# Tiles 2 and 3 turned by VectorE, h in three float32r passes, the sums of T on GpSimd, and a reordered start of a residual conditioning kernel

## The reference

```python
# x (128, 128, 512), cond (128, 512), weight_matrix (1024, 512), W_proj (512, 512), b_proj (512,)
u = gelu(cond @ W_proj + b_proj, approximate=False)
W_u, W_e = weight_matrix[:512], weight_matrix[512:]
out = x + (u @ W_u)[:, None, :] + einsum('bnd,dc->bnc', x, W_e)
```

## Time and profile before

| | |
|---|---|
| time, median of 3 runs | 346.73 us (346.72 to 347.13) |
| time of the profiled execution | 347.7 us, its span 345.4 us |
| TensorE busy | 339.6 us, 98% of the span |
| TensorE weight loads | 328.7 us, 95% |
| VectorE / ScalarE / GpSimd busy | 261.7 / 247.0 / 277.2 us (76 / 72 / 80%) |
| DMA | 70.64 MB, mean 205 GB/s |
| granted TensorE clock | 1.00 in every stretch |

### The profile page before, as it was taken

The page is one execution under the profiler, slowest core; times in us unless marked ns, Lnnn a source line. Parts: engine busy times, 40 slices in busy tenths (PEclk is TensorE's granted clock), DMA queues, the critical chain, the costliest instruction groups (busy, mean ns, idle before and its releaser), DMA issues.

```text
span 345.4 us, 7856 instructions
## 1 busy us (share of the span) xinstructions
PE 339.6 (98%) x2706; PEld 328.7 (95%) x2706; DVE 261.7 (76%) x301; ACT 247.0 (72%) x424; POOL 277.2 (80%) x196
## 2 busy tenths in 40 slices
PE   7999999999999999999999999999999999999996
PEld 3758999999999999999999999999999999999996
DVE  2869977788777778877777897777789777778811
ACT  3646877877777787777778777777877777787741
POOL 0357998888989888898988889898888989888860
PEclk9999999999999999999999999999999999999999
DMA  7998697888799788879978887997887799788116
GB/s 257 331 180 236 123 238 201 221 194 204 176 228 241 195 219 196 198 180 229 237 200 218 195 197 178 232 233 202 219 197 197 175 235 237 197 209 210 83 56 228
DMA packets 72264, 70.64 MB, mean 205 GB/s; under 512 B 2880, under 2 KB 67392, under 8 KB 68032
## 3 DMA queue, kind: packets, MB, share of 16 engines
q1 hardware_dynamic: 72256, 70.53, 80.5%
HBM read 36.96 MB, written 33.55 MB: 204 GB/s over the span
## 4 chain that ended last, share of the span: by engine, by line
PE 89%; DVE 1%; ACT 0%; issue 0%
PE banks L743 30%; PE banks L747 29%; PE banks L745 29%; DVE work L509 1%; DVE banks L509 0%; DVE banks L552 0%; ACT snap_rows L461 0%; ACT y L504 0%; ACT hi L399 0%
## 5 line engine op out<-in xcount | busy, mean ns | idle before, releaser
L743 PE MATMUL banks<-t_hi,hi 128*128 128x256 f32 x496 | 140.5, 283 | 0.2 <-ACT snap_rows L461 0.2
L745 PE MATMUL banks<-t_lo,hi 128*128 128x256 f32 x496 | 140.4, 283 | 0.0
L747 PE MATMUL banks<-t_hi,lo 128*128 128x256 f32 x496 | 140.4, 283 | 0.0
L743 PE MATMUL banks<-w_hi,hi 128*128 128x256 f32 x372 | 105.3, 283 | 0.4 <-ACT banks L424 0.4
L745 PE MATMUL banks<-w_lo,hi 128*128 128x256 f32 x372 | 105.3, 283 | 0.0
L747 PE MATMUL banks<-w_hi,lo 128*128 128x256 f32 x372 | 105.3, 283 | 0.0
L509 DVE STREAM_TRANSPOSE work<-quad_raw 128x1024 f32<-128x1024 f32 (+1 forms) x62 | 100.7, 1624 | 3.6 <-DMA quad_raw<-in_x 3.6
L743 PEld LDWEIGHTS banks<-t_hi,hi 128*128 128x128 f32 x496 | 95.2, 192 | 0.6 <-issue 0.6
L747 PEld LDWEIGHTS banks<-t_hi,lo 128*128 128x128 f32 x496 | 95.2, 192 | 0.0
L745 PEld LDWEIGHTS banks<-t_lo,hi 128*128 128x128 f32 x496 | 95.2, 192 | 0.0
L316 POOL TENSOR_TENSOR lo<-work,hi 128x1024 fp32r<-128x1024 f32 x31 | 74.8, 2413 | 21.7 <-ACT hi L391 21.7
(11 more groups left out here) (71 smaller groups left out, 401.7 us busy)
## 6 DMA issues: line engine op xcount, KB each, us to landing
out<-y SPq DMA_DIRECT2D x31, 1024.0 KB, 4.5
quad_raw<-in_x SPq DMA_DIRECT2D x120, 256.0 KB, 5.7
head_raw<-in_x SPq DMA_DIRECT2D x2, 512.0 KB, 5.7
w_e<-in_L_cond_weight_matrix SPq DMA_DIRECT2D x2, 512.0 KB, 6.2
w_proj_sb<-in_L_cond_W_proj SPq DMA_DIRECT2D x1, 1024.0 KB, 10.0
w_u<-in_L_cond_weight_matrix SPq DMA_DIRECT2D x1, 1024.0 KB, 12.3
quad_raw<-in_x SPq DMA_DIRECT2D x8, 128.0 KB, 9.5
out<-y SPq DMA_DIRECT2D x3, 256.0 KB, 2.1
```

The source lines that it names most:

```text
L743: pe.matmul(psum[:, t, :], a_hi[:, 2 * j + t, :], b_hi[:, j, :], start=False, stop=False, skip_group_check=True)
L745: pe.matmul(psum[:, t, :], a_hi[:, 2 * j + t, :], b_lo[:, j, :], start=False, stop=False, skip_group_check=True)
L747: last = pe.matmul(psum[:, t, :], a_lo[:, 2 * j + t, :], b_hi[:, j, :], start=False, stop=(j == T - 1), skip_group_check=True)
```

## The change

- **Loads.** Tiles 2 and 3 are no longer loaded by one DMA of 4 KB rows behind W_e, but by four DMAs in 512-byte pieces (`second`), behind cond and W_proj. W_proj is loaded in two halves.
- **Turning.** Tiles 2 and 3 are turned by VectorE straight into PSUM (`turn_second`); TensorE's eight flips of them are gone.
- **h.** `cond_t @ W_proj` in float32 becomes three float32r passes of four matmuls each. ScalarE casts `proj_hi` (four) and `cond_hi`, VectorE makes `proj_lo` (four) and `cond_lo`; they lie in the buffers hi[0] and lo[0], so the first casts of quad 0 wait for `h_summed`.
- **GpSimd.** The identity is added to three of the four diagonals by GpSimd, and the four sums of T are made by GpSimd, after `proj_lo`. `split_t(3)` moves behind the first split of `prepare`.
- **VectorE.** S3 of quad 0 goes ahead of S2, the lo part of S1 behind the bias; `turn_up` of quad 1 goes between the two evacuations. The bias copy waits for `a_seeded`.
- **ScalarE.** `seed_a` of quad 0 reads the bias from PSUM and goes ahead of `hi_s2`, `seed_c` ahead of `hi_s3`. In `period(0)` `seed_c` of quad 1 goes behind `snap5`, and `hi_s1` of quad 1 behind `snap2`.
- **TensorE.** One more warm-up matmul; the hi·hi matmuls of tiles 0 and 1 run one j ahead. The result banks are dealt out otherwise: quad 0's A bank is now bank 7 and its C bank is bank 6.

```diff
-WARM_UP = 6
+WARM_UP = 7
...
+        proj_hi, proj_lo = of_proj(hi[0]), of_proj(lo[0])
+        cond_hi, cond_lo = of_cond(hi[0]), of_cond(lo[0])
...
+        direct = head_raw[:, 0:T * TILE].rearrange("p (n d) -> p n d", n=T)
+        second = head_raw[:, T * TILE:HEAD * TILE].rearrange("p (m n w) -> p m n w", m=NM, n=T)
...
-        a_bank = [bank(6).rearrange("p (t c) -> p t c", t=T), bank(2).rearrange("p (t c) -> p t c", t=T)]
-        c_bank = [bank(1).rearrange("p (t c) -> p t c", t=T), bank(3).rearrange("p (t c) -> p t c", t=T)]
+        a_bank = [bank(7).rearrange("p (t c) -> p t c", t=T), bank(2).rearrange("p (t c) -> p t c", t=T)]
+        c_bank = [bank(6).rearrange("p (t c) -> p t c", t=T), bank(3).rearrange("p (t c) -> p t c", t=T)]
...
+            return w_e[:, j, :].rearrange("p (a r) -> p a r", r=NJ)[:, :, j]
...
-            load_direct(0)
+            sp.dma_start(direct, x[:, 0:T, :]).then_inc(direct_loaded, 16)
             for n in range(2):
                 load_w_e(n)
-            load_direct(1)
             sp.dma_start(cond_sb[:, :], cond).then_inc(cond_loaded, 16)
-            sp.dma_start(w_proj_sb[:, :, :], w_proj_dram).then_inc(w_proj_loaded, 16)
+            for n in range(2):
+                sp.dma_start(w_proj_sb[:, 2 * n:2 * n + 2, :],
+                             w_proj_dram[:, 2 * n:2 * n + 2, :]).then_inc(w_proj_loaded[n], 16)
+            for q in range(NQ):
+                sp.dma_start(second[Q * q:Q * (q + 1)], x_dram[q, :, :, T:HEAD, :]).then_inc(second_loaded, 16)
...
+            pool.wait_ge(ident_ready, 1)
+            for j in range(1, NJ):
+                pool.wait_ge(w_e_loaded[j // 2], 16)
+                diag = diagonal(j)
+                pool.tensor_tensor(diag, diag, ident[:, :], ALU.add).then_inc(w_diag_ready, 1)
...
-            for n in range(4):
-                split_t(n)
+            b_of = w_e[:, :, :].rearrange("p (e j) (h c) -> p e h j c", e=2, h=2)
+            b11, b12, b21, b22 = b_of[:, 0, 0], b_of[:, 0, 1], b_of[:, 1, 0], b_of[:, 1, 1]
+            pool.wait_ge(proj_lo_ready, NJ)
+            pool.wait_ge(w_diag_ready, NJ - 1)
+            pool.wait_ge(first_diag_ready, 1)
+            pool.tensor_tensor(t_sum[:, 0, :, :], b12, b11, ALU.subtract).then_inc(t_summed, 1)
+            pool.tensor_tensor(t_sum[:, 2, :, :], b22, b12, ALU.subtract).then_inc(t_summed, 1)
+            pool.wait_ge(t_summed, 1)
+            pool.tensor_tensor(t_sum[:, 1, :, :], b22, t_sum[:, 0, :, :], ALU.subtract).then_inc(t_summed, 1)
+            pool.wait_ge(t_summed, 3)
+            pool.tensor_tensor(t_sum[:, 3, :, :], b21, t_sum[:, 1, :, :], ALU.subtract).then_inc(t_summed, 1)
...
                 if first:
+                    split_t(3)
                     split_s2()
                     sum_s4()
                 else:
@@ -341,6 +377,8 @@
...
+            for n in range(3):
+                split_t(n)
             prepare(0, 0, True)
...
-                act.wait_ge(direct_flipped, n + 1)
+                if n < T:
+                    act.wait_ge(direct_flipped, n + 1)
+                else:
+                    act.wait_ge(second_turned, n - T + 1)
...
             for n in range(T):
                 direct_hi(n)
             for j in range(1, NJ):
-                act.wait_ge(w_diag_ready, j + 1)
+                act.wait_ge(w_diag_ready, j)
                 act.copy(w_hi[:, j, :], w_e[:, j, :]).then_inc(w_hi_ready[j], 1)
-            for n in range(T, HEAD):
-                direct_hi(n)
+            for j in range(NJ):
+                act.wait_ge(w_proj_loaded[j // 2], 16)
+                act.copy(proj_hi[:, j, :], w_proj_sb[:, j, :]).then_inc(proj_hi_ready, 1)
+            act.wait_ge(cond_flipped, 1)
+            act.copy(cond_hi, flip_psum).then_inc(cond_hi_ready, 1)
...
             hi_t(0)
-            act.wait_ge(cond_flipped, 1)
-            act.copy(cond_t[:, :, :], flip_psum).then_inc(cond_ready, 1)
-            for n in range(1, 4):
-                hi_t(n)
+            for n in range(T, HEAD):
+                direct_hi(n)
             act.wait_ge(h_summed, 1)
             act.copy(h[:, :], h_psum).then_inc(h_ready, 1)
+            hi_t(1)
             act.wait_ge(h_flipped, 1)
             act.wait_ge(b_proj_loaded, 16)
             for j in range(NJ):
                 last = act.activation(u_t[:, j, :], flip_psum[:, j, :], ACT.Gelu, bias=b_proj_sb[:, j:j + 1])
             last.then_inc(u_ready, 1)
+            hi_t(2)
+            hi_t(3)
...
+                elif p == 0:
+                    act.wait_ge(h_summed, 1)
...
             def seed_a(k, p, first):
+                source = bias
+                if not first:
+                    act.wait_ge(c21_out, k - 1)
+                elif p == 0:
+                    act.wait_ge(h_ready, 1)
+                    act.wait_ge(bias_summed, 1)
+                    source = bias_psum
+                else:
+                    act.wait_ge(bias_ready, 1)
+                    act.wait_ge(evacuated, HEAD_CHUNKS)
+                act.copy(a_bank[p], source[:, left].unsqueeze(1).to_broadcast([P, T, H])).then_inc(a_seeded, 1)
...
+            def seed_c(k, p, first):
...
                 early = first and p == 0
+                if ahead and not early:
+                    seed_c(k + 1, 1 - p, early)
                 if ahead:
-                    seed_c(k + 1, 1 - p, early)
                     up(k + 1, 1 - p, early)
...
                 if ahead:
+                    if early:
+                        seed_c(k + 1, 1 - p, early)
                     seed_a(k + 1, 1 - p, early)
-                    hi_s1(k + 1, 1 - p, early)
+                    if not early:
+                        hi_s1(k + 1, 1 - p, early)
                 act.wait_ge(m6_done, k + 1)
                 if not first:
                     act.wait_ge(c12_out, k - 1)
                 act.copy(snap2[p][:, :, :], a_bank[p]).then_inc(snap2_taken, 1)
+                if ahead and early:
+                    hi_s1(k + 1, 1 - p, early)
...
             hi_a22(0, 0, True)
+            seed_a(0, 0, True)
             hi_s2(0, 0, True)
+            seed_c(0, 0, True)
             hi_s3(0, 0, True)
-            seed_a(0, 0, True)
-            seed_c(0, 0, True)
...
+            def turn_second(t):
+                transpose(direct_psum[t].rearrange("p j (i m) -> p m j i", m=NM),
+                          second[:, :, t, :].rearrange("p m (k j) -> p m j k", k=Q)).then_inc(second_turned, 1)
...
-            dve.wait_ge(w_diag_ready, 1)
+            dve.wait_ge(w_e_loaded[0], 16)
+            first_diag = diagonal(0)
+            dve.tensor_tensor(first_diag, first_diag, ident[:, :], ALU.add).then_inc(first_diag_ready, 1)
+            dve.wait_ge(first_diag_ready, 1)
             dve.tensor_copy(w_hi[:, 0, :], w_e[:, 0, :]).then_inc(w_hi_ready[0], 1)
             split_direct(0)
-            add_identity(1)
             split_direct(1)
-            add_identity(2)
-            add_identity(3)
             for j in range(NJ):
                 split_w(j)
-
-            b_of = w_e[:, :, :].rearrange("p (e j) (h c) -> p e h j c", e=2, h=2)
-            b11, b12, b21, b22 = b_of[:, 0, 0], b_of[:, 0, 1], b_of[:, 1, 0], b_of[:, 1, 1]
-            dve.wait_ge(w_diag_ready, NJ)
...
+            for j in range(NJ):
+                dve.wait_ge(proj_hi_ready, j + 1)
+                dve.tensor_tensor(proj_lo[:, j, :], w_proj_sb[:, j, :], proj_hi[:, j, :].bitcast(F32),
+                                  ALU.subtract).then_inc(proj_lo_ready, 1)
+            dve.wait_ge(cond_hi_ready, 1)
+            dve.tensor_tensor(cond_lo, flip_psum, cond_hi.bitcast(F32), ALU.subtract).then_inc(cond_lo_ready, 1)
+            dve.wait_ge(second_loaded, LOADS)
+            dve.wait_ge(direct_lo_ready, T)
+            for t in range(T):
+                turn_second(t)
             for n in range(T, HEAD):
                 split_direct(n)
             turn_up(0, 0, True)
             turn_low(0, 0, True)
             sum_s1(0, 0, True)
+            sum_s3(0, 0, True)
             sum_s2(0, 0)
-            split_s1(0, 0)
-            sum_s3(0, 0, True)
+            dve.wait_ge(a_seeded, 1)
             dve.wait_ge(bias_summed, 1)
             dve.tensor_copy(bias[:, :], bias_psum).then_inc(bias_copied, 1)
             dve.wait_ge(bias_copied, 1)
             dve.tensor_tensor(bias_step[:, :], bias_psum[:, right], bias[:, left], ALU.subtract).then_inc(bias_ready, 1)
+            split_s1(0, 0)
             evacuate(0)
+            turn_up(1, 1, True)
             evacuate(1)
-            turn_up(1, 1, True)
...
+            def high(j):
+                pe.wait_ge(w_hi_ready[j], 1)
+                for t in range(T):
+                    if j == 0:
+                        pe.wait_ge(direct_hi_ready, t + 1)
+                    product(t, x_hi[0], w_hi, j, first=(j == 0))
...
+            high(0)
             for j in range(NJ + 1):
+                if j + 1 < NJ:
```

(54 more changed lines are left out.)

27 lines of the change are left out of this document (5 added, 22 removed).

## The result

The changed kernel takes 345.77 us (median of 8 runs, 345.43 to 346.81) against 346.70 us before (8 runs); the ratio of the two is 0.997, 95% interval 0.9956 to 0.9984: it is 0.3% faster, where I forecast no change.

A forecast was written before the change was run, and what follows sets the result against it. TensorE, gapless from m7 of quad 0, was taken to bound the kernel. Loads +1.68 us and order -1.53 us gave +0.15 us on the 346.73 median: 346.9 us, likeliest case 346.1 to 347.4, 8-in-10 range 345.6 to 347.7.

The forecast's parts named there:

- Steady part and tail untouched, the end moves with m7 of quad 0: TensorE runs without a gap from product m7 (old start counted as 36.77 us); the end moves as much as m7.
- TensorE done with tile 3 between 27.2 and 28.4: TensorE's start-up list: 1.4 us shorter, less up to 1.2 us from GpSimd's additions meeting VectorE; 28.66 before.
- The path from T to m6, 9.13 us: Quad 0, from VectorE's start on its lower half, through casts, GpSimd's S4 and ScalarE's copy, to TensorE's product m6.
- The order's gain of 1.53 us: Start of quad 0: with the old loads, the new order of work would start m7 1.53 us earlier.
- The price of the loads on the path, 1.68 us: Queue ahead of quad 0: 1.12 us for slower 512-byte pieces plus 0.56 us for a changeover, all delaying its landing.
- The 0.56 us for the changeovers: Loads: a change from large rows to pieces passes only 159 GB/s against 221, losing 0.12 MB, 0.56 us.
- Now 23.40: New time in us at which VectorE starts on quad 0's lower half, 1.68 us later than 21.72.
- T by 22.5: Sign against the forecast: VectorE starting on quad 0's lower half by 22.5 us would show it wrong.
- T = 21.72: Time in us at which VectorE started transposing quad 0's landed lower half (into A21) in the kernel before.
- That the kernel before follows T: In the kernel before, m7's start hangs on the chain from quad 0's load through S1 and snap2, ending 35.96 us.
- the loads are not later: Rival: pieces cost no more than rows, quad 0 lands as before, m7 starts at 35.6, time 345.5 us; chance 0.26.
- Margins: Small slacks in other lists: 0.13 us at GpSimd before m1 of quad 1, 0.5 us at snap2 before m7.

The follow-up runs named there:

- e4: The changed kernel with four more warm-up matmuls (0.85 us in all) on TensorE just ahead of h: 345.80 us, ratio 0.9976.
- e7: The changed kernel with S1's cast of quad 1 ahead of the copy snap2 again: 346.90 us, ratio 1.0003.
- e12: The changed kernel with both evacuations ahead of turn_up of quad 1 again: 346.21 us, ratio 0.9971.
- e9: The changed kernel with quad 0's old order on VectorE and ScalarE, plus eight warm-up matmuls on TensorE behind tile 3: 347.53 us, ratio 1.0014.
- e2: The kernel before with tiles 2 and 3 loaded in 512-byte pieces at their old place in the queue, values laid out wrongly: 347.58 us, ratio 1.0028.
- e6: The kernel before with only W_proj's load split into two halves: 346.73 us, ratio 0.9996.
- e3: The changed kernel with quad 0's work on VectorE and ScalarE back in its old order: 348.36 us, ratio 1.0033.
- e5: The kernel before, unchanged, run once more for a second profile: 346.86 us, ratio 1.000.
- e10: The changed kernel with ScalarE's copy into B's bank moved ahead of S4's cast: 345.96 us, ratio 0.9956.

## Why the prediction was wrong

- **Steady part and tail untouched, the end moves with m7 of quad 0.** Right: m7 came 1.76 us earlier (36.70 to 34.94; 1.83 with the restart), the last matmul 1.83, the span 1.8.
- **TensorE done with tile 3 between 27.2 and 28.4.** Slightly too dear: it was done at 26.92. GpSimd's additions of the identity (three, where I had counted two) took 0.68 us for one and 1.01 for the other two, near the 0.5 us each of the slope. The meeting that was to cost up to 1.2 us hardly took place: GpSimd's last addition ended at 8.96 and VectorE's four split_w began at 8.81. What did meet GpSimd's first addition (6.73 to 7.41) was VectorE's own addition, 0.39 us as in the kernel before, and its cast of W_e, 0.43 us there and 0.58 here. The forecast's ends were 28.4 and 27.2, and it came out by the second. The first was also what the Trainium skill, "SBUF — State Buffer", section "SBUF: two separate sides", would have made of it. The changed kernel's trace doesn't test that rule for the additions against split_w, which overlap by 0.15 us at most.
- **The path from T to m6, 9.13 us.** Right: 9.06, and 9.1 in e4, e7 and e12. The order's gain of 1.53 us was right in size too: 1.5 at a given T in e9, and e1, the changed kernel with its loads in rows, is 1.58 us faster than the kernel before. That the second figure fits so well is partly luck, for in e1 GpSimd's list sets the end and not T.
- **The price of the loads on the path, 1.68 us, is the step that failed.** It is the larger term of the sum (1.68 - 1.53 = +0.15), and it measured about a third to a half of that: 0.55 us by the medians of e1 and the changed kernel (0.31 by m7), and 0.8 us in the old order (e2). With 0.55 in its place the sum is about -1.0, and -0.93 was measured. Two things were wrong in it. The 0.56 us for the changeovers rested on the dip to 159 GB/s in the earlier trace rows; in the same window the second profile of that kernel shows 202, e6 230 and the changed kernel 339, so most of the dip belongs to one execution. And the rest was put on the path whole, though the change itself had given GpSimd the sums of T. In the forecast GpSimd was done with them at 23.4, before up was cast at 24. In the changed kernel up is cast by 22.35 and its lo part still starts at 22.66, and no earlier with the rows of e1; all the slack left behind that is the 0.39 us of idle time ahead of 26.71, which caps what an earlier landing can bring. How much later the pieces land is not settled: 1.45 us in one pair, 0.8 by the means.
- **"Now 23.40" was 1.9 us off**, and by the prediction's own sign (T by 22.5) this alone says that it was wrong. The changed kernel starts at 21.49; in seven relatives with pieces T was between 20.9 and 21.6, in e3 22.5. Besides the price, the base was late: T = 21.72 came from an execution whose own time was 1 us above its kernel's median. A late base explains why T didn't move between the two traces. It explains little of the error in the time, because the old m7 (36.77) came from the same late trace: both sides of the sum were late together.
- **That the kernel before follows T.** Right in three of four profiles (T + 15.0 to 15.1), and incomplete: e5 has T 1.6 us earlier than the first and the same end, by way of TensorE's list, tile 3 and the second evacuation. So in the kernel before too, an earlier landing pays only down to where that list lies. The change takes both paths away from snap2: TensorE's by the shorter list and by turn_up between the evacuations, T's by snap2 ahead of the cast.
- **The rival that won, *the loads are not later*,** won for another reason than its own. The Trainium skill, "DMA: Bandwidth & Descriptors", section "Specifications", puts line rate at 512 bytes and above; 221 GB/s against 420 in the earlier trace rows stays against it. The pieces do pass more slowly and probably land later, but only 0.3 to 0.55 us of it lie on the path (e1), since GpSimd's sums of T are in the way.
- **Margins.** GpSimd's lo of up of quad 1 was 0.21 us ahead of TensorE in the forecast (0.13 with the semaphore) and 0.19 us in the trace; e10 shows it as the next limit.

Open: what slowed the flips and warm-up matmuls in e5, and with it how often the kernel before takes which of its two paths; how much later the pieces land; what each part of the change gives alone in the kernel before, the new dealing of the result banks among them.

## What to carry to other kernels

A transfer that gets slower costs the time only as far as no other list holds its reader back: before its whole price goes on the path, look at what else the reader waits for, above all at work that the same change has moved there (here GpSimd's sums of T). Before a landing time or a dip in bandwidth from one profile enters a sum, look where that execution's own time stands in the kernel's runs, and take a second profile of the same kernel: here the landing varied by 1.6 us, more than what was to be foretold. Where two lists meet at one wait, price both to their ends; the earlier one shows no wait and is easily taken for slack. When a stall is left in front of a product, look in the releasing engine's list for something that could stand behind the release, and then at once for the next list whose margin is smaller than the gain.

## What the hardware showed beyond that

TensorE's granted clock fell to half, 1.2 GHz, from about 31.4 to 34.8 us after a wait of 2.54 us at 27.4 to 29.9 us, and matmuls of 256 columns went from one every 0.12 us to one every 0.21 (e3; six of its nine executions have the lower mean clock). Waits of 0.8 to 1.1 us (the changed kernel, e7) left it at 1.00, and filling all but 0.81 us of the same wait with matmuls kept it at 1.00 too (e9). Loads from DRAM in pieces of 512 bytes ran at 213 to 249 GB/s (16 to 23 us in all fourteen profiles, 11 to 13 us in the nine with tiles 2 and 3 in pieces behind W_proj), rows of 2 KB and more at 390 to 426 (7 to 13 us in the four profiles with rows), with the DMA engines busy in both.
